# A decoder of two layers on one core: four sets of batch buffers, decay tiles per batch, maxima moved by small DMAs

## What is computed

```
h = x + mixer(layernorm(x))              # state space: 16 decays, a causal convolution of 256 steps each
h = h + attention(norm(h), context)      # x0: 16 heads of 8, 64 keys
h = h + moe(attention(norm(h), itself))  # s0: 16 heads of 4, 256 keys; then 8 experts, the best 2 weighted
h = h + attention(rms(h), itself)        # s1: 16 heads of 8, 4 heads of keys, 256 keys
h = h + attention(norm(h), context)      # x1: as x0, with rotary positions
y = h + mlp(norm(h))                     # 128 -> 512 -> 128
```

## Time and profile before

| | |
|---|---|
| median of three runs | 728.47 us |
| the profiled execution, first to last instruction | 728.7 us (only its span is recorded) |
| TensorE (PE) busy | 634.2 us, 5800 matmuls |
| VectorE (DVE) busy | 550.5 us, 1513 instructions |
| ScalarE (ACT) busy | 438.1 us, 863 |
| GpSimd (POOL) busy | 178.4 us, 348 |
| granted TensorE clock, mean | 0.988 |
| first step of TensorE's list | at 27 us |

### The profile page before, as it was taken

One profiled execution on the slowest core, in us unless ns is written; L12 is line 12 of the kernel. 1 busy time (PEld: TensorE's weight loads), 2 busy tenths in 40 slices (PEclk: granted clock), 3 DMA queues, 4 the chain that ended last, 5 costly groups with the idle time before them and its releaser, 6 DMA issues.

```text
span 728.7 us, 14858 instructions
## 1 busy us (share of the span) xinstructions
PE 634.2 (87%) x5800; PEld 430.9 (59%) x5800; DVE 550.5 (76%) x1513; ACT 438.1 (60%) x863; POOL 178.4 (24%) x348
## 2 busy tenths in 40 slices
PE   2688899899799998899888997978999899999887
PEld 0255458458556685558645684554567467674556
DVE  7559986858987789776878468899758965777783
ACT  4124666675676646756577544756775678767534
POOL 9614411102132222211241033051132102020202
PEclk9989999999999999999999999999999999999999
DMA  8400000000000000000000000000000000000000
GB/s 298 119 2 9 1 1 1 2 1 1 1 22 2 2 9 7 9 1 1 16 2 1 1 2 15 2 1 1 2 16 2 1 1 1 1 1 2 2 1 22
DMA packets 10358, 10.62 MB, mean 15 GB/s; under 512 B 2832, under 2 KB 9520, under 8 KB 10032
## 3 DMA queue, kind: packets, MB, share of 16 engines
q1 hardware_dynamic: 9568, 6.98, 3.3%
q10 hardware_dynamic: 720, 2.69, 0.9%
HBM read 8.60 MB, written 1.07 MB: 13 GB/s over the span
## 4 chain that ended last, share of the span: by engine, by line
PE 49%; DVE 32%; ACT 11%; issue 4%; POOL 2%; DMA 1%; ACTq 1%; SPq 0%; POOLq 0%; DVEq 0%
DVE qs L1150 8%; PE psA L1562 8%; PE psB L1549 8%; PE psO L1500 6%; ACT P L839 5%; PE psB L1476 4%; PE psA L1460 4%; PE psM L1439 4%; DVE QT L1138 4%; DVE qs L1145 3%; PE psM L1358 3%; PE psM L1315 2%; ACT QT L836 2%; DVE stats L948 1%; DVE kz_s L1131 1%
## 5 line engine op out<-in xcount | busy, mean ns | idle before, releaser
L839 ACT ACTIVATE P<-psB 128x512 f32<-128x512 f32 x320 | 176.9, 597 | 71.5 <-PE psB L1476 46.1
L1150 DVE TENSOR_REDUCE qs<-psA 128x2 bf16<-128x512 f32 x256 | 165.4, 690 | 26.6 <-PE psA L1460 25.4
L1460 PE MATMUL psA<-kz_s,QT 128*128 128x512 bf16 x256 | 90.7, 385 | 13.7 <-DVE qs L1150 8.0
L1476 PE MATMUL psB<-QT,kz_s 128*128 128x256 bf16 x512 | 90.6, 276 | 9.7 <-ACT QT L836 3.2
L846 ACT ACTIVATE P<-psB,W 128x256 f32<-128x256 f32 x160 | 66.4, 473 | 39.8 <-PE psB L1549 34.8
L1439 PE MATMUL psM<-identb,qs 128*128 128x128 bf16 x896 | 72.4, 222 | 11.0 <-DVE qs L1145 2.9
L1439 PEld LDWEIGHTS psM<-identb,qs 128*128 128x128 bf16 x896 | 56.3, 99 | 31.6 <-issue 8.0
L1500 PE MATMUL psO<-P,vp 128*32 128x256 f32 x1024 | 68.3, 385 | 2.1 <-ACT P L839 1.5
L1476 PEld LDWEIGHTS psB<-QT,kz_s 128*128 128x128 bf16 x512 | 39.2, 98 | 52.2 <-ACT P L839 26.3
L1562 PE MATMUL psA<-w,P 128*128 128x128 f32 x512 | 66.1, 277 | 1.8 <-ACT P L846 0.9
L661 POOL TENSOR_SCALAR veps<-mv 128x2 f32<-128x2 f32 x40 | 10.4, 261 | 229.2 <-DVE mv L952 228.6
(11 more groups left out here) (178 smaller groups left out, 1109.8 us busy)
## 6 DMA issues: line engine op xcount, KB each, us to landing
w<-expert_w ACTq DMA_DIRECT2D x2, 1024.0 KB, 10.3
toep<-decay_rows SPq DMA_DIRECT2D x4, 512.0 KB, 5.9
x<-x SPq DMA_DIRECT2D x8, 128.0 KB, 2.8
y<-base SPq DMA_DIRECT2D x8, 128.0 KB, 1.9
W<-weights SPq DMA_DIRECT2D x1, 940.0 KB, 6.9
rows<-bias_rows SPq DMA_DIRECT2D x1, 872.0 KB, 10.4
ctxp<-context SPq DMA_DIRECT2D x8, 64.0 KB, 2.1
fw<-mlp_w ACTq DMA_DIRECT2D x2, 256.0 KB, 10.9
```

The costliest lines, as they stand in the source:

```text
L839: act.activation(P[:, p, :, :].rearrange("p a s -> p (a s)"), psB[:, s.u % B_BANKS, :], ACT.Exp, scale=LAYERS[s.L]["scale"]).then_inc(b_dr ...
L1150: dve.tensor_reduce(qs[L["W"]][j][:, t * H + h:t * H + h + 2, 0], ps.rearrange("p (h c) -> p h c", h=2), AX.X, ALU.max, negate=True).then_ ...
L1460: ins = pe.matmul(ps, QT[j][:, h // L["HB"], t * 128:t * 128 + 128], kz[s.L][j][:, kv:kv + 2, :].rearrange("p h s -> p (h s)"), start=True ...
L1476: ins = pe.matmul(ps[:, i * S:i * S + S], kz[s.L][j][:, kv + i, kc * 128:kc * 128 + 128], QT[j][:, h // L["HB"], :], start=True, stop=True)
```

## The change

`SLOTS` becomes 4, and all strings of `ORDER` are new; SP gets a string of its own, with 75 steps. What makes room for the fourth set: the q tile qs exists twice (`Q_SETS = 2`) and the turned keys of s0 three times (`K_SETS = 3`) for all batches, handed on in the order of the list; the split keys of s0 have one tile, kn, those of s1 and the contexts another, kw; xm shares xnT, on4 is gone, bias rows are kept once and not twice; and of the 16 decay tiles only four stay. The other twelve (`RESIDENT = 3` parts) are loaded again for each batch, into its places of P and into QT, when the batch before in that set is done. T4 now waits for all parts.

The maxima no longer go through qs. VectorE's reduction writes them to a small tile, negmax; M is one transpose of 128x16, one copy of 16x128, and one DMA on SP's queue that puts the 16 rows into QT. S waits for that DMA. P3 clears the two columns in s0 alone. POOL waits before it splits keys until the tile's last ones are turned, ScalarE's P3 likewise for the q set. The strings of POOL, SP and the opening exponentials (now in P) are left out below.

```diff
-SLOTS = 3
+SLOTS = 4
+Q_SETS = 2
+K_SETS = 3
+RESIDENT = 3
...
+    if engine == "SP" and s.kind == "M":
+        out[f"max_moved{s.j}_{s.q}"] = 16
...
+    keys = [y for y in order["PE"] if y.kind == "K" and y.L == "s0"]
+    for n, s in enumerate(keys):
+        s.kset = n % K_SETS
...
+    splits = [y for y in order["ACT"] if y.kind == "P3"]
+    for n, s in enumerate(splits):
+        s.qset = n % Q_SETS
+        s.turned_q = find(batches[splits[n - Q_SETS].b], "Q", splits[n - Q_SETS].L, 1) if n >= Q_SETS else None
...
-        toep = sb("toep", [128, NS, S])
+        toep = sb("toep", [128, NS - 4 * RESIDENT, S])
...
+        def decay_home(j, n):
+            if n < 2:
+                return P[:, P_SLOTS * j + 2 * n:P_SLOTS * j + 2 * n + 2, :, :].rearrange("p a b s -> p (a b) s")
+            return queries[j][:, :, :] if n == 2 else toep[:, :, :]
...
+            def load_decay(b):
+                j = b % SLOTS
+                for n in range(RESIDENT):
+                    sp.dma_start(decay_home(j, n), decay_part(n)).then_inc(decay_loaded[j], 16)
...
-            for n in range(4):
-                sp.dma_start(toep[:, 4 * n:4 * n + 4, :],
-                             bass.AP(decay.tensor, 4 * n * (128 + S), [[1, 128], [128 + S, 4], [1, S]])).then_inc(toep_loaded[n], 16)
-            for s in order["DVE"]:
+            for n in range(RESIDENT, NS // 4):
+                sp.dma_start(decay_home(0, n), decay_part(n)).then_inc(rest_loaded, 16)
+            for b in range(SLOTS):
+                load_decay(b)
+            for s in order["SP"]:
+                if s.kind == "M":
+                    m, f, b, c = s.misc
+                    sp.wait_ge(misc_drained[m], c)
+                    groups = groups_of(s)
+                    sp.dma_start(QT[s.j][0:128:LAYERS[s.L]["W"], groups[0]:groups[0] + len(groups), :],
+                                 negmaxT[s.j][:, s.q, :]).then_inc(max_moved[s.j][s.q], 16)
...
                     if s.b + SLOTS < B:
                         load_x(s.b + SLOTS)
+                        load_decay(s.b + SLOTS)
...
+                if s.kind == "M":
+                    m = free(s)
+                    act.copy(negmaxT[j][:, s.q, :], bf(m)[0:16, 0:128]).then_inc(misc_drained[m], 1)
...
-            for j in range(SLOTS - 1):
-                blank(j)
+            blank(blocks[:6])
...
-                    mark(dve.memset(tile[:, :, 0:MS], 0.0))
                     if ahead(q_part1, s.after["q_part1"]):
                         dve.wait_ge(q_part1, s.after["q_part1"])
+                    if s.L == "s0":
+                        mark(dve.memset(tile[:, :, 0:MS], 0.0))
...
+                    if ahead(decay_loaded[j], 16 * RESIDENT * (s.b // SLOTS + 1)):
+                        pe.wait_ge(decay_loaded[j], 16 * RESIDENT * (s.b // SLOTS + 1))
                     for n in range(NS // 4):
-                        if ahead(toep_loaded[n], 16):
-                            pe.wait_ge(toep_loaded[n], 16)
...
+                if s.kind == "M":
+                    a = previous(s, "A", s.L, 2 * s.q + 1 if L["cross"] else 8 * s.q + 7).a
+                    if ahead(a_drained, a + 1):
+                        pe.wait_ge(a_drained, a + 1)
+                    m = take(s)
+                    pe.transpose(bf(m)[0:16, 0:128], negmax[j][:, s.q, :], identb[:, :]).then_inc(misc_filled[m], 1)
...
                 if s.kind == "S":
-                    drained(previous(s, "M", s.L, s.q // 2 if L["cross"] else s.q // 8))
+                    half = s.q // (2 if L["cross"] else 8)
+                    moved = previous(s, "M", s.L, half).after[f"max_moved{j}_{half}"]
+                    if ahead(max_moved[j][half], moved):
+                        pe.wait_ge(max_moved[j][half], moved)
```

More of the change, by code:

```diff
@@ L260, in user, with number @@
     return find(batch, "H", s.L, s.q if s.L == "s0" else 0)
-def number(batches, order):
+def number(batches, contexts, order):
     fills, drains = [0, 0], [0, 0]
@@ L290, in number @@
             o += 1
+    place = {y: n for n, y in enumerate(order["PE"])}
+    keys = [y for y in order["PE"] if y.kind == "K" and y.L == "s0"]
+    for n, s in enumerate(keys):
+        s.kset = n % K_SETS
+        assert n < K_SETS or place[find(batches[keys[n - K_SETS].b], "S", "s0", 15)] < place[s]
+    splits = [y for y in order["ACT"] if y.kind == "P3"]
+    for n, s in enumerate(splits):
+        s.qset = n % Q_SETS
+        s.turned_q = find(batches[splits[n - Q_SETS].b], "Q", splits[n - Q_SETS].L, 1) if n >= Q_SETS else None
+    last = {}
+    for s in order["POOL"]:
+        if (s.kind == "C" and s.q == 0) or (s.kind == "P3" and not is_cross(s)):
+            tile = "kn" if s.L == "s0" else "kw"
+            s.turned_k = last.get(tile)
+            last[tile] = find(contexts[s.b // 2], "C", s.L, 1) if s.kind == "C" else find(batches[s.b], "K", s.L)
     for engine, steps in order.items():
@@ L300, in decoder @@
     batches, contexts, order = schedule()
-    number(batches, order)
+    number(batches, contexts, order)
     with ExitStack() as ctx:
@@ L370, in decoder @@
         on = both("on", [128, T, D])
-        on4 = both("on4", [128, T, D])
         xn2 = on
@@ L422, in decoder @@
         ot_drained = [sem(f"ot_drained{o}") for o in range(2)]
+        max_moved = [[sem(f"max_moved{j}_{half}") for half in range(2)] for j in range(SLOTS)]
         weights_loaded = sem("weights_loaded")
@@ L516, in query_block, with maxima @@
             return QT[s.j][:, groups[0]:groups[0] + n, :].rearrange("p g s -> p (g s)"), bf(m)[:, 0:n * S]
+        def maxima(s):
+            L, half, n = LAYERS[s.L], s.q // (2 if is_cross(s) else 8), H // LAYERS[s.L]["HB"] // 2
+            tile = negmax[s.j][:, half, :]
+            if L["cross"]:
+                lo = s.q % 2 * 4
+                return tile.rearrange("p (a m) -> p a m", a=L["HB"])[:, :, lo:lo + 4]
+            h, t = scores_of(s)
+            lo = h // L["HB"] % n * T + t
+            return tile.rearrange("p (a m) -> p a m", a=L["HB"])[:, h % L["HB"]:h % L["HB"] + 2, lo]
         def bf(m):
@@ L567, in _ @@
                     load_context(s.b // 2 + 1)
-                if s.kind == "H" and s.L == "f":
+                if s.kind == "H":
                     store(s)
```

230 lines of the change are left out of this document (124 added, 106 removed).

## The result

The changed kernel takes 723.59 us (median of 11 runs, 721.1 to 728.96), the kernel before 729.55 in the same runs; the ratio is 0.9922, with a 95% interval of 0.9895 to 0.9948. So it is faster, by 5.7 us (in what follows a ratio is turned into us by 729.5). Forecast were 698.4 us and at most 720: the sign was right, the size was not.

The account below looks back on a forecast made before the run. TensorE's in-order stream was taken to set the pace, with idle time from drains; -19.4 - 5.4 - 1.9 + 5.6 + 4.5 + 2 + 2 - 17.7 = -30.3 us on 728.7 gave 698.4 us, range 674 to 720.

Parts of the forecast that it names:

- Decay tiles, +2 and +2: Decay loads for each batch: +2 us for T4 of batch 0 at the opening, +2 us for later loads ahead of moves.
- That hides: Opening decay transfers for batches 1 and 2 land at 43 and 48 us, claimed to cost T4 no time.
- Removed transposes, -19.4: TensorE's step M: 384 fewer transposes at 57 ns, 21.9 us of stream, counted at 89%: -19.4 us.
- drains, -7.3: Smaller copies behind M and fewer memsets: -5.4 us for VectorE and -1.9 us for ScalarE, by chain shares.
- Work taken from TensorE should come back nearly whole: TensorE's stream sets the pace, so its removed work returns nearly whole, other engines' work by their share of the chain.
- The busy share of 89%: TensorE busy for 621.5 of the 701.7 us behind the opening 27 us; used to price the removed transposes.
- Table loads, +5.6: ScalarE switches between Exp and Gelu: 22 more loads, 28.2 us, counted by the chain's share, 5 of 25: +5.6 us.
- The rival that they are paid in full: ScalarE's added table loads all count: +22.6 us on the forecast, 721 us; chance 0.05.
- The +4.5: S waiting for moves of maxima, 2.4 us from M: 13.0 us uncovered in the new list against 8.4 in the old.
- the slower rival: Moves come late at each first S: 742 us with a 3.5 us landing, 763 with 4.0; chance 0.09.
- The fourth set, -17.7: TensorE's waits: 3.67 batches under way instead of 2.86 hide 22% of 80.2 us idle: -17.7 us.
- The shared tiles, costed at nothing: Two q sets, three of keys, one k tile per width: 0 us; if they bind, the fourth set's gain goes.

Follow-up runs that it names:

- the context first: Changed kernel, but SP loads the second pair's context right behind batch 0's decay tiles, ahead of those of batches 1 to 3: 716.1 us, 0.9793.
- idle stretches filled: Changed kernel with 150 matmuls on constants where TensorE sat idle: 712.91 us, 0.9774; the kernel before with 106: 728.52 us, 0.9985.
- the run with the small M and no move: Kernel before, old order and three sets, with one transpose and small copy for M, no transfer of maxima: 723.68 us, 0.9891.
- both repairs: Changed kernel with the second pair's context loaded earlier and later decay loads behind next moves: 712.74 us, 0.9773; batch 7's loads after one move: 707.48 us, 0.9685.

## Why the prediction was wrong

Two steps failed that experiments on the changed kernel itself show. The sum listed of SP's queue only what the moves and T4 need, and it had no term for the clock. With the context first, the later decay loads behind the next move and the idle stretches filled, the changed kernel runs at 0.9637: 26.5 us under the kernel before, where 30.3 were forecast and 5.7 measured. These edits leave the transposes, the copies, the moves, the table loads and the four sets as they are, and give 20.8 of the 24.6 us that are missing (the kernel before would gain 1.1 of them by filled gaps too).

**Decay tiles, +2 and +2: 7.4 for the later reload alone, and 9.4 for a stall that was in no term.** "That hides" was said of T4, and SP's next duty, the context of batches 2 and 3, wasn't looked at. Thirteen parts stood before it, TensorE waited 7.7 us, and 9.4 us are won by moving it. The same holds at the hand-over: it was costed by the moves behind the loads, while x of a later batch stands behind them too. The first +2 was right in itself (T4 waited 1.97 us), but the wait for the context behind it takes it in. The step to fault is that not everything behind the decay loads on that queue was listed with who needs it first. The prediction had cited the rule of the Trainium skill (DMA: Bandwidth & Descriptors, HWDGE ordering) that each DMA engine takes descriptors in ring order, and the landings agreed; it was applied to the moves alone.

**The clock: no term.** The sum took the clock as given. It is the other thing missed: 62 us at half speed in the profiled run, and 10.8 us of time. In the 11 runs of the changed kernel, time at half speed goes from 58 to 76 us, and a least-squares line through them gives 0.41 us of span for each (correlation 0.96). The filled gaps gave back only 0.17 for each. A longer wait lengthens both the span and the time at half speed, and the added matmuls may cost something themselves; which of the two makes the difference is not shown, so 10.8 us is what is measured, with the matmuls' own cost in it.

**Removed transposes, -19.4, and drains, -7.3: less, and how much less depends on the order.** "Work taken from TensorE should come back nearly whole" failed in the old order: the two terms were worth 8.0 us by themselves (10.1 with the gaps filled) where 26.7 were taken. The busy share of 89% was read as if the rest of the list moved up with it; the trace shows other waits grow in its place. In the new order the same transposes, put back, cost 14.5 us, and 17 to 21 apart from the clock, which is near the 19.4. The drains were not put back there, so their worth in the new order is open.

**Table loads, +5.6: none.** The rival that they are paid in full is out too. The count (22 more) was right, the share of the chain wasn't a price. The likely reading, not shown, is that a load on the chain is there because ScalarE happened to be last, and that without it something else ends at nearly the same time.

**Moves: 9.7 for 13.0.** The +4.5 was 13.0 us uncovered in the new order less 8.4 for the old copies, and those 8.4 are in the run with the small M and no move, where the waits for copies fell from 6.9 us to 2.9. So 9.7 is to be set against 13.0, and this part was about right. The landing was faster than assumed (1.6 us for 2.0), so the slower rival, which needed 3.2 us, was far off; what the term lacked is in the chain: moves of 3.0 to 4.3 us at the hand-over. Without the new order the moves would have cost some 53 us (1.0617 against 0.9891), which the count of steps between M and S foretold well (about 60 us).

**The fourth set, -17.7.** Not measured alone, since the changed order can't be run with three sets. With the old order's worth of the removed work, what is left is: -8.0 of removed work, +9.7 of moves, +9.4 of context and +7.4 of reload make +18.5, and the result is -5.7. So order and fourth set together gave about 24 us with the clock's loss in it, and about 34 if that loss (10.8 less 1.1, some 10 us) is counted apart. With the 14.5 us that the transposes cost in the new order in place of 8.0 it is about 18 and 28. It is a remainder of terms that overlap (each repair also shortens the time at half speed: 66 us at the mean of the runs, 56 with the context first, 44 with both repairs), so it stays an estimate, and that the 18 is close to the 17.7 forecast proves nothing. The shared tiles, costed at nothing, show once in the trace of the changed kernel: POOL waits once for the wide k tile kw, 9.4 us up to 98.2 us; ScalarE never waits for a q set. What that one wait costs was not tried. The stretches bear it out in kind: idle time fell in the middle and rose at both ends and the hand-over, of which the prediction named the hand-over as what spoke against.

By the old order's 8.0 the miss of about 25 us (30.3 less 5.7) would be: the removed work with the old waits overrated by 27, the clock 10, the context stall 9, the decay tiles 3 more than costed; on the other side the moves 3, the table loads 6 and order with fourth set some 16 more than their term. As the last is a remainder, these come to the miss by the way they are made, and don't confirm it. What stays open is how much of the removed work came back in the new order, and with it the worth of the fourth set.

## What to carry to other kernels

When transfers are added to a queue, list everything behind them with its first user, not only what the change is about: here a context, moves and an x load. Removed busy time need not be removed time in a kernel whose orders are laid out by hand: ask, for the engine that is relieved, what its next step waits for, or measure the removal alone before costing it, and in the order that it will run in. And look at the clock row as at a resource: a change that bunches idle time can lose in the clock what it wins in work, and useless matmuls in the gaps can be worth more than they cost.

## What the runs showed of the hardware

Both times below, TensorE's granted clock fell while the engine was idle or right behind it. Stretches of the changed kernel around two of its falls:

```profile
...
42.00:43.00 1.00, 0.06 (x1) 0.00 (x0) 0.87 (x2) 0.00 (x0) 0.00 (x0) 1.00 1.09 387
44.00:46.00 2.00, 0.00 (x0) 0.00 (x0) 0.00 (x0) 0.00 (x0) 0.00 (x0) 0.50 1.09 385
...
42.00:50.00 8.00, 0.31 (x2) 0.26 (x2) 0.91 (x2) 0.00 (x0) 0.00 (x0) 0.59 0.81 276
50.00:58.00 8.00, 6.96 (x46) 5.43 (x50) 3.31 (x15) 1.77 (x3) 2.34 (x4) 0.50 0.00 0
395.00:405.00 10.00, 5.98 (x71) 4.49 (x69) 8.85 (x28) 1.98 (x3) 1.77 (x4) 1.00 0.62 192
405.00:409.00 4.00, 3.97 (x20) 3.11 (x20) 1.93 (x7) 1.54 (x3) 0.19 (x1) 0.57 0.91 247
...
```

It fell within the idle stretch from 42.05 to 49.74 us (1.00 up to 43, 0.50 from 44 on), and stayed at 0.50 until 58 us, though TensorE was busy for 6.96 of the last 8; and it fell at 405 us, behind 10 us with 5.98 busy, of which the last 2.5 were a wait for a move. With the gaps filled the mean over the span was 0.997 to 1.000 in the profiled runs of four kernels and 0.991 in that of the fifth. By regression within each kernel a us at half speed goes with 0.2 to 0.5 us of span, 0.31 over all of them; what came back when the gaps were filled is 0.07 to 0.18 us for each. Both are less than the half us of work that TensorE loses in it (but for one kernel at 0.53).

SP's issue slowed behind large transfers under way: in the opening, decay parts are issued in 0.38 to 0.63 us each for the first five and in 1.2 to 2.1 us from the sixth on, so SP itself was held until 42.8 us, and its later duties with it. An x load of 128 KB took 6.06 us behind three decay parts and 2.16 without them. And 4 KB within the on-chip memory land in 1.6 us, less than the 1.9 to 2.1 of the earlier trace rows.
